# Causal attention scores as fp32 products of 32 rows on four row groups, three score buffers, no bf16 split

## The reference, cut to what matters

```python
H, D, C1, C2 = (16, 32, 256, 128)          # heads, width of a head; here B = 2, S = 1024
q = jnp.einsum('bsc,hcd->bhsd', xn, wq)
k = jnp.einsum('btc,hcd->bhtd', yn, wk)
v = jnp.einsum('btc,hcd->bhtd', yn, wv)
a = jax.nn.softmax(jnp.einsum('bhsd,bhtd->bhst', q, k) * D ** (-0.5), axis=-1)
if causal:
    s, t = (a.shape[-2], a.shape[-1])
    mask = (jnp.arange(t)[None, :] > jnp.arange(s)[:, None]).astype(a.dtype)
    a = a * mask
o = jnp.einsum('bhst,bhtd->bhsd', a, v)
```

## Time and profile before

| | |
|---|---|
| median of 3 runs | 2523.2 us |
| the profiled execution, its own time | 2524.3 us |
| its span, first to last instruction | 2522.6 us |
| mean granted TensorE clock | 0.902 |
| PE busy | 2047.2 us (81%) |
| DVE busy | 1367.6 us (54%) |
| ACT busy | 929.6 us (37%) |
| POOL busy | 710.5 us (28%) |

### The profile page before, as it was taken

The page is one execution under the profiler, slowest core; times in us unless marked ns, Lnnn a source line. Parts: engine busy times, 40 slices in busy tenths (PEclk is TensorE's granted clock), DMA queues, the critical chain, the costliest instruction groups (busy, mean ns, idle before and its releaser), DMA issues. The chain is left out here.

```text
span 2522.6 us, 36317 instructions
## 1 busy us (share of the span) xinstructions
PE 2047.2 (81%) x11904; PEld 1504.7 (60%) x11904; DVE 1367.6 (54%) x3511; ACT 929.6 (37%) x1859; POOL 710.5 (28%) x1199
## 2 busy tenths in 40 slices
PE   5983974467867677999799979969898589999991
PEld 4661863354444454555455558846687378888991
DVE  4871006535745765888688847757636432222332
ACT  4220321112324346888688843232232112222230
POOL 0223011030130125777577751102330230000005
PEclk9995995578979789999999989979999699999995
DMA  2004531000011286333333430110000525555684
GB/s 87 1 1 150 167 104 28 13 13 14 1 19 12 82 216 165 85 85 85 86 65 92 97 108 11 28 36 1 1 13 1 193 104 175 175 175 175 215 287 115
DMA packets 171504, 219.20 MB, mean 87 GB/s; under 512 B 39911, under 2 KB 133540, under 8 KB 165184
## 3 DMA queue, kind: packets, MB, share of 16 engines
q1 hardware_dynamic: 163344, 196.65, 26.7%
q0 software_dynamic: 7264, 20.31, 2.5%
q10 hardware_dynamic: 720, 0.07, 0.0%
HBM read 171.13 MB, written 46.14 MB: 86 GB/s over the span
## 5 line engine op out<-in xcount | busy, mean ns | idle before, releaser
L2390 DVE TENSOR_REDUCE l3s_mx<-banks 128x1 f32<-128x1024 f32 x256 | 313.1, 1223 | 96.7 <-PE banks L2292 93.8
L2292 PE MATMUL banks<-l_stack 128*128 128x512 bf16 x1024 | 268.1, 385 | 44.1 <-ACT xn_tokens L2373 21.0
L1012 PE MATMUL banks<-l3f_xrt,l3f_w 128*128 128x256 f32 (+1 forms) x1536 | 277.9, 342 | 2.7 <-issue 1.5
L1012 PEld LDWEIGHTS banks<-l3f_xrt,l3f_w 128*128 128x128 f32 x1536 | 249.6, 192 | 29.1 <-issue 3.3
L1302 DVE TENSOR_SCALAR l3f_sg<-banks 128x256 f32<-128x256 f32 (+1 forms) x192 | 72.0, 375 | 287.5 <-PE banks L1012 287.5
L2273 POOL TENSOR_TENSOR xn_tokens<-xn_tokens,l3s_sm 128x1024 f32<-128x1024 f32 (+3 forms) x128 | 201.6, 1575 | 50.3 <-DVE l3s_sm L2397 49.2
L222 PE MATMUL banks<-ident,xn_tokens 128*128 128x128 f32 x320 | 64.7, 338 | 166.8 <-DVE xn_tokens L211 148.0
L2292 PEld LDWEIGHTS banks<-l_stack 128*128 128x128 bf16 x1024 | 80.8, 98 | 163.3 <-ACT xn_tokens L2373 52.6
L2373 ACT ACTIVATE xn_tokens<-banks,l3s_mx 128x1024 f32<-128x1024 f32 x128 | 142.7, 1115 | 46.2 <-DVE l3s_mx L2390 45.1
L222 PEld LDWEIGHTS banks<-ident,xn_tokens 128*128 128x128 f32 x320 | 46.6, 172 | 188.4 <-DVE xn_tokens L211 133.0
L2373 ACT ACTIVATE x_features<-banks,l3s_mx 128x1024 f32<-128x1024 f32 x128 | 143.0, 1117 | 27.9 <-DVE l3s_mx L2390 27.6
(11 more groups left out here) (532 smaller groups left out, 3925.4 us busy)
## 6 DMA issues: line engine op xcount, KB each, us to landing
l3f_w<-in_L_ffn_gate_up_w_dram SPq DMA_DIRECT2D x24, 2048.0 KB, 7.6
l3f_w<-in_L_ffn_down_w_dram SPq DMA_DIRECT2D x24, 1024.0 KB, 6.0
l_stack<-l_q_part SPq DMA_DIRECT2D x72, 256.0 KB, 6.0
l_stack<-l_k_part SPq DMA_DIRECT2D x72, 256.0 KB, 11.4
l0f_w<-in_L_ffn_W_dram SPq DMA_DIRECT2D x16, 1024.0 KB, 5.8
l_q_part<-l_stack SPq DMA_DIRECT2D x24, 256.0 KB, 3.0
l_k_part<-l_stack SPq DMA_DIRECT2D x24, 256.0 KB, 3.7
l3f_rows<-l3f_zero SPq DMA_DIRECT2D x13, 384.0 KB, 4.1
```

The source lines that it names most:

```text
L1012: last = nc.tensor.matmul(ps[:, f % 4, h * PAIR:h * PAIR + size], w1_sb[:, p, dc, h * FF + f * P:h * FF + (f + 1) * P], xrt[:, p, dc, 0:si ...
L2292: last = nc.tensor.matmul(ps[:, 2 * (v % 2) + h, :], stack[p][0][s][:, r, si * P:(si + 1) * P], stack[p][1][s][:, r, h * 512:(h + 1) * 512 ...
L2390: nc.vector.tensor_reduce(mx[:, v % RING:v % RING + 1], ps[:, 2 * (v % 2):2 * (v % 2) + 2, :].rearrange("p a n -> p (a n)"), AX_X, ALU.max ...
```

## The change

It has four parts.

1. q and k are no longer split: the projection stage stores fp32 banks, q by ACT and k by DVE, and POOL has nothing to do in it. The scratch has fp32 q and k, the extra entry is gone, and an entry takes 9 loads instead of 17.
2. Scores are fp32 matmuls of 32 rows. One call makes the scores of two heads: four matmuls of 512 columns, on the four row groups of the array (queries of a head stand twice in 64 partitions, beside the two halves of its keys), into four of six score banks. There are three score buffers (banks 0 to 5), and the call for units v and v+1 waits for the exponential of unit v-2.
3. The turned chunks and the outputs now share banks 6 and 7, in the order of use (`uses`). All chunks of an output window are multiplied in one piece at its first unit, and it waits until every earlier use of either bank is stored. ACT stores results in bank 6, DVE in bank 7; the output's copy stands ahead of the next exp or maximum. The hardware loop is gone: all 8 entries are written out.
4. `narrow` is true for width 32 too, so the cross attention `l3a` takes the narrow form.

```diff
@@ -350,7 +350,7 @@
     HK = HEADS * KEYS
     chunks = HEADS * width // P
     per = P // width
-    narrow = width * 4 <= KEYS
+    narrow = width * 2 <= KEYS
...
-SLOTS = (((0, 0, 1, 1), (0, 1, 0, 1)),
-         ((0, 2, 1, 2), (2, 0, 2, 1)))
-LOADS = 2 * 2 * 4 + 1
+LOADS = 2 * GROUP + 1
...
-    stack = [[[ctx.enter_context(nc.sbuf_tensor(f"l3_stack{p}{kind}{s}", [P, GROUP, TOK], BF16)) for s in range(2)]
-              for kind in range(2)] for p in range(2)]
+    queries = ctx.enter_context(nc.sbuf_tensor("l3_queries_in", [P, 2, GROUP // 2, TOK], F32))
+    keys = ctx.enter_context(nc.sbuf_tensor("l3_keys_in", [P, 2, GROUP // 2, TOK // 2], F32))
...
+    (q_scratch, k_scratch), v_scratch, _ = scratch
+    loaded, queries, keys, values = entry
+    for m in range(GROUP):
+        rows_of, odd, half = slice(m * L3_WIDTH, (m + 1) * L3_WIDTH), m // 2, m % 2
+        q_head, k_head = (src[n].rearrange("(a o d) n -> o d a n", o=2, d=L3_WIDTH)[odd] for src in (q_scratch, k_scratch))
+        sp.dma_start(queries[rows_of, p], q_head).then_inc(loaded[p], 16)
+        sp.dma_start(keys[rows_of, p], k_head[:, :, half * TOK // 2:(half + 1) * TOK // 2]).then_inc(loaded[p], 16)
+    sp.dma_start(values[:, p], v_scratch[n]).then_inc(loaded[p], 16)
...
+    SENDS = 4
...
+        qk = sb("qk", [P, 2, 2 * BANKS, 512])
...
+                    for kind, stored in ((0, q_stored), (1, k_stored)):
+                        sp.wait_ge(stored, BANKS * (k + 1))
+                        sp.dma_start(
+                            q_k_scratch[kind][entries, :, at:at + PAIR].rearrange("g p n -> p g n"),
+                            qk[:, p, kind * BANKS:(kind + 1) * BANKS, :].rearrange(
+                                "p m (g n) -> p (m g) n", n=PAIR)).then_inc(sent[p], 16)
...
-            @block.gpsimd
-            def _(pool):
-                for k in range(PAIRS):
-                    for m in range(2 * BANKS):
-                        pool.wait_ge(mid_made, 2 * BANKS * k + m + 1)
-                        nc.gpsimd.tensor_tensor(parts[k % 2][2][:, m, :], rest[:, m, :], parts[k % 2][1][:, m, :],
-                                                ALU.subtract).then_inc(low_made, 1)
...
-                        high(k, 0)
-                        for m in range(1, 2 * BANKS):
-                            high(k, m)
-                            mid(k, m - 1)
-                        mid(k, 2 * BANKS - 1)
+                        if k >= 2:
+                            act.wait_ge(sent[k % 2], sent_before(k))
+                        for m in range(BANKS):
+                            act.wait_ge(qk_ready, 2 * BANKS * k + m + 1)
+                            nc.scalar.activation(qk[:, k % 2, m, :], ps[:, m, :], ACT.Copy,
+                                                 scale=L3_WIDTH ** -0.5).then_inc(q_stored, 1)
                         for u in range(2):
...
-                    nc.vector.scalar_tensor_tensor(rest[:, m, :], ps[:, m, :], L3_WIDTH ** -0.5 if m < BANKS else 1.0,
-                                                   parts[k % 2][0][:, m, :], ALU.mult, ALU.subtract).then_inc(rest_made, 1)
+                def store_keys(k):
+                    if k >= 2:
+                        dve.wait_ge(sent[k % 2], sent_before(k))
+                    for m in range(BANKS, 2 * BANKS):
+                        dve.wait_ge(qk_ready, 2 * BANKS * k + m + 1)
+                        nc.vector.tensor_copy(qk[:, k % 2, m, :], ps[:, m, :]).then_inc(k_stored, 1)
...
+    SCORES = 3
+
+    uses = {}
+    for v in range(ENTRIES * UNITS + OUT):
+        if TURN <= v < ENTRIES * UNITS + TURN:
+            for g, group in enumerate(groups):
+                if group[0] == (v - TURN) % UNITS:
+                    uses["turn", (v - TURN) // UNITS, g] = len(uses)
+        if v >= OUT and (v - OUT) % R == 0:
+            uses["out", (v - OUT) // R] = len(uses)
+
+    def stored_through(side, n):
+
+        return (n + 2 - side) // 2
...
-        with nc.Fori(0, ENTRIES // BODY) as jj:
...
-                    def scores(v):
-                        p, si, r = v // UNITS % 2, tile_of(v), v % R
-                        if v >= 2:
-                            pe.wait_ge(exped, v - 1)
...
+                def scores(v):
+                    p, si, pair = v // UNITS % 2, tile_of(v), v % R // 2
+                    if v >= SCORES - 1:
+                        pe.wait_ge(exped, v - SCORES + 2)
+                    for u in range(2):
                         for h in range(2):
-                            for s in range(2):
-                                last = nc.tensor.matmul(ps[:, 2 * (v % 2) + h, :],
-                                                        stack[p][0][s][:, r, si * P:(si + 1) * P],
-                                                        stack[p][1][s][:, r, h * 512:(h + 1) * 512],
-                                                        start=(s == 0), stop=(s == 1))
-                        last.then_inc(scores_ready, 1)
...
+                            lanes = slice((2 * u + h) * W, (2 * u + h + 1) * W)
+                            last = nc.tensor.matmul(ps[:, 2 * ((v + u) % SCORES) + h, :],
+                                                    queries[lanes, p, pair, si * P:(si + 1) * P],
+                                                    keys[lanes, p, pair, :], start=True, stop=True)
+                    last.then_inc(scores_ready, 1)
...
-                    def output(w, q):
...
-                        chunks = [c for c in range(si, KC) if (c - si) % R == q]
-                        if q == 0:
...
+                def output(w):
+                    e, si = w // KC, ORDER[w % KC]
+                    n = uses["out", w]
+                    for side in range(2):
+                        pe.wait_ge(stored[side], stored_through(side, n - 1))
+                    for c in range(si, KC):
+                        for r in range(R):
+                            last = nc.tensor.matmul(ps[r * W:(r + 1) * W, 6 + n % 2, 0:P],
+                                                    values[:, e % 2, c, r * W:(r + 1) * W],
+                                                    pt[:, w % 2, r, c - si, :], start=(c == si),
+                                                    stop=(c == KC - 1))
+                    last.then_inc(out_ready, 1)
...
+                    if v < ENTRIES * UNITS and v % 2 == 0:
+                        scores(v)
+                    if TURN <= v < ENTRIES * UNITS + TURN:
+                        turn(v - TURN)
+                    if v >= OUT and (v - OUT) % R == 0:
+                        output((v - OUT) // R)
...
+            def store_output(eng, op, v, side):
+
+                if v < OUT or (v - OUT) % R != 0:
+                    return
+                w = (v - OUT) // R
+                e, si = w // KC, ORDER[w % KC]
+                if uses["out", w] % 2 != side:
+                    return
+                eng.wait_ge(out_ready, w + 1)
+                if e >= 2:
+                    eng.wait_ge(out_sent[e % 2], 16 * (e // 2))
+                dst, src = heads_out[:, e % 2, si * P:(si + 1) * P], ps[:, 6 + side, 0:P]
+                last = op.activation(dst, src, ACT.Copy) if side == 0 else op.tensor_copy(dst, src)
...
+            @block.vector
+            def _(dve):
+                for v in range(ENTRIES * UNITS + OUT + 1):
+                    store_output(dve, nc.vector, v - 1, 1)
+                    if v < ENTRIES * UNITS:
+                        dve.wait_ge(scores_ready, v // 2 + 1)
+                        nc.vector.tensor_reduce(mx[:, v % RING:v % RING + 1],
+                                                ps[:, 2 * (v % SCORES):2 * (v % SCORES) + 2, :].rearrange("p a n -> p (a n)"),
+                                                AX_X, ALU.max, negate=True).then_inc(measured, 1)
...
```

305 lines of the change are left out of this document (111 added, 194 removed).

## The result

The changed kernel takes **2542.4 us** (median of 4 runs, 2540.42 to 2544.32), the kernel before 2522.9 (4 runs beside it, 2519.68 to 2523.38). The ratio is 1.008 with a 95% interval from 1.0063 to 1.0097: slower by 16 to 24 us.

What follows compares the result with a forecast made beforehand. A circle between PE, DVE and ACT in attention was taken to bound the kernel. Attention +32, clock +8, projection -25 and l3a 0 made +15 us, so 2538; the forecast's bounds were 2516 to 2585, the stated range 2475 to 2605.

Steps and rivals of the forecast that it cites:

- The call: Attention, PE: four fp32 score matmuls side by side take 0.98 us; the maximum on DVE begins 1.18 us after the start.
- fewer abreast: Rival, attention calls: row groups run two at a time (+109 us, 2648) or one at a time (+311, 2850); chance 0.08.
- A pair without an output: Attention: two units with no output behind their call take 3.71 us, the circle of call, maximum and exp.
- A pair with an output: Attention: output waits for unit v-5's copy behind the maximum, begins about 2.85 us after the call; next call at 4.65.
- The attention stage: Whole attention stage: 549.5 us against 517, so +32 us, plus +8 us for a lower clock.
- The seam: Attention in the kernel before: the hardware loop's seam costs 16.3 us, which the changed stage no longer has.
- The clock: Attention: granted clock falls to 0.97 as some stretches lose it, +8 us; bounds 0 and +65 at 0.84.
- the clock falls: Rival, attention: PE's short pieces and waits bring the stage's clock to the projection stage's 0.84, 2596 us; chance 0.10.
- Projection: Projection stage: DVE sets the pace, 11.9 us per pair; PE ends at 932.5, tail 3 us shorter; -25 us.
- l3a: Cross attention l3a: pairs of tiles +3, folds -4.5, longer tail +1.5, sum 0; bounds -5 and +6 us.
- The fast rival: Attention: the output is out of the way, all pairs take 3.71 us, -26 in this stage, 2473; chance 0.12.
- half of it: Attention: half of the fast rival, the wait costs 0.45 us per output, 2503 us; chance 0.10.

Runs made afterwards that it cites:

- Loosened: The changed kernel, but an output waits only for the stored copies it reads and the bank use it overwrites: 2495.0 us, ratio to before 0.989.
- one_chunk: The changed kernel with only the last chunk of each output multiplied, the wait ahead of outputs kept: 2511.0 us.
- two_buffers: The changed kernel with a call for units v and v+1 waiting for the exponential of unit v, as with two score buffers: 2881.6 us.
- two_groups: The changed kernel with a call's four products on two row groups, both units using the first head's rows: 2850.3 us.

## Why the prediction was right, and where it was off

The case that came is the forecast's: slower, by a wait ahead of the outputs. The sum was +15 us against 16.1 between the profiled executions. (The median is 4 over the 2538 because this profiled execution lies 2.0 under the median of its runs, where that of before lay 1.1 over it.) The terms were less exact than the sum, and that it came so close is luck: attention was 12.8 us above its terms, and projection (4.9), l3a (3.5) and a stage that nobody touched (2.9) were as much below.

- **The call (0.98 us, 1.18 on the way to DVE).** Measured 1.07 and 1.21. Right in kind: four abreast, and the runs with one and two row groups show what fewer would cost. The rival "fewer abreast" falls. The Trainium skill (TensorE: Matmul & The Clock Gate, Measured speedup vs the span model) gives 3.07x, from which the prediction's estimate was 1.11 us. The trace has 3.3x and 1.07 us, which lies between that and my 0.98.
- **A pair without an output (3.71 us).** Measured 3.72 to 3.73.
- **A pair with an output (4.65 us).** Measured 4.85. The mechanism was named rightly, down to the line: the copy of unit v-5 behind the maximum. The start of the output failed in size, 2.85 us after the call predicted, 3.04 measured on average, and that is the whole difference: the call is longer, and 0.15 us pass between the copy's end and the output, which the sum didn't have. Over 64 outputs it makes 13 us: an entry takes 68.6 us and not 67. (The 0.1 that the prediction adds for the queue stands in neither its 4.65 nor its 8.36.)
- **The attention stage (+32 and +8 of clock).** Measured +52.8, 13 more than these 40: +13 by the outputs' start, +2 by a head and tail of 20.4 us instead of 18.8, less 2 of clock and of the pipe's fill. The seam, 16.3, is worth 14.5 by itself.
- **The clock (+8 us, at 0.97).** The granted clock was right (0.97 from 938 to 1506), and so was its price within 2 us. Two dips cost 1.5 and 1.6 us: the window of 10.10 us instead of 8.65 in the first entry, and the fifth entry's 70.2 us instead of 68.6. The rest stands at the stage's start, which is at 1.2 GHz from 935.3 to 955.8: the first two windows, which have no output yet, take 9.35 and 9.09 us instead of the 7.45 that two pairs take at full clock. (With all key copies by ACT this stretch is 13.7 us long, and there the second window does take 7.45.) Together 6.6 us. Windows of the two dips, and of a quiet stretch ahead of the second:

```profile
962.90:966.30 3.40, 3.31 (x64) 3.17 (x64) 1.14 (x2) 0.99 (x2) 2.04 (x3) 0.54 0.02 5
...
1225.00:1239.00 14.00, 9.45 (x97) 5.51 (x98) 11.44 (x21) 10.50 (x19) 8.51 (x15) 1.00 0.48 107
1239.40:1242.80 3.40, 3.40 (x61) 2.83 (x57) 0.58 (x2) 0.79 (x4) 1.44 (x2) 0.54 0.91 309
```

  Both dips fall into an output of eight chunks that PE waited 1.4 us for; the second takes 3.46 us instead of 1.95. The rival "the clock falls" did not come, but it was nearer than its 0.10 looked: one more wait, or shorter work, brought this stage to 0.63 and 0.92. Neither the dips nor the long start were foreseen by place; 0.97 was a guess at their sum.
- **Projection (-25 us).** Measured -29.9. The working holds to the end of PE's products: last norm 910.5 predicted, 910.9 measured; PE's end 932.5 and 932.2; the pair 11.9 and 12.1. That DVE sets the pace is shown by the run with its copies taken away. The step that failed is the tail: I took 3 us off the 12.2 ahead of attention, and 7.3 went, since 4.87 is left. By the program neither POOL's last subtractions nor the sends of the bf16 parts stand there any more; how the 7.3 divide between them was not tried.
- **l3a (0).** Measured -3.5 between the two profiles. Folds -4.6 (predicted -4.5). The wait for `heads` came as predicted, 16.45 us for two tiles (16.55). What I had left out is two things. The tiles without a normed pair gain 0.5 each, and the last products come a tile later, so the third and fourth steps between tiles are 3.2 us shorter and the tail is +4.1 instead of +1.5. The steady part is -3.0 instead of +3: +1.9 in the four pairs of tiles with a normed pair, -1.9 in the three steps ahead of them, and that -3.2, of which some 0.8 is a clock stretch of the kernel before. The stage between, not touched, was 2.9 us shorter in this execution; in the twelve profiles it takes 178.3 to 181.3 us.
- **The fast rival (2473, or half of it 2503).** It decided at an output start under about 1.6 us after the call. In the change no output starts before 2.78. Loosened, those with 1.33 to 1.66 cost nothing, as that rival has it, and the kernel takes 2495. Its mechanism was real and one wait's index away.

The loosened kernel also gives an account between old and new design. Between the profiles of the kernel before and of this one lie 29.6 us. Attention begins 31.3 us earlier (29.4 of it in the projection stage), the stage behind it and l3a take 5.2 less, and the attention stage takes 525.6 us instead of 518.5, 7.1 more. In these 7.1 are **+18** for the attention entries (8 x (63.4 - 61.1)), -14.5 for the seam and +3.5 for its first two windows at 1.2 GHz. Against the kernel before with its loop written out, whose stage takes 502.7 us, it is +22.9. Even without the needless wait the new attention stage is slower than the old one without its seam; the version pays by what it takes out of the projection stage.

## What to carry to other kernels

When two kinds of use share a pair of buffers in one order, "everything earlier is stored" is an easy way to write a wait, and it makes a consumer wait for copies that it neither reads nor overwrites; ask what stands ahead of the last such copy on its engine. Taking a sixth of the work off PE brought nothing here: with the tight wait an entry took 68.6 us, and with the wait as loose as the data allow 63.4, where the kernel before had 61.1. Measure the parts of a large change apart: here the loop's seam, a part that needs none of the rest, was worth 14 us by itself.

## What the runs showed that I had not expected

The granted clock doesn't follow PE's busy share over a stage. In this stage: 92% busy and 0.99 in the kernel before; 71% and 0.98 in the change; 70% and 0.92 with outputs of one chunk; 69% and 0.63 with calls that wait longer; 86% and 0.64 with two row groups; 93% and 0.54 with one. When the clock fell it cost more than the edit itself: with one row group 470 us beyond the 311 of the serial calls.

But a busy share at a low clock is misleading, since the same products take twice as long at 1.2 GHz (a call on one row group 7.12 us, against 3.63 at full clock). Three stretches at full clock, of `one_chunk`, `two_buffers` and `two_groups`:

```profile
1314.90:1386.60 71.70, 48.15 (x380) 24.39 (x378) 59.47 (x108) 55.95 (x105) 50.49 (x72) 1.00 0.15 38
```

```profile
1297.00:1303.80 6.80, 3.32 (x25) 1.63 (x25) 3.39 (x7) 3.56 (x8) 3.24 (x6) 1.00 1.05 214
```

```profile
1152.50:1179.80 27.30, 21.43 (x175) 11.55 (x171) 17.02 (x29) 16.37 (x31) 15.49 (x21) 1.00 0.26 56
```

Counted over all parts of the stage at full clock, without its first and last two windows, PE is busy for 94% in the kernel before and 71% in the change (each with 0.99 of the clock over the same stretch), 77% in the loosened kernel (1.00), 69% and 67% with outputs of one chunk, without and with the wait (0.96 and 0.93), and 42% with two buffers (0.64). Among the kernels that use four row groups, the less PE had to do at full clock, the lower was the clock. The runs on fewer groups stand outside this order: 79% and 0.64 with two, and 99% and 0.54 with one, of which only 89 us are at full clock. The longest single pause of PE there is no guide: 1.45 us in the change and with outputs of one chunk alike, 1.43 with two groups, 1.20 with one, 2.90 with two buffers. Which part the rows of the array have in that, and which the rhythm of calls and waits, was not tried.
